# Cross-attention kernel, first layer: how the turned probabilities are copied out of PSUM, and the order of work at the layer's two ends

## What is computed

```python
q = hidden @ Wq + bq                    # 32 heads x 16
k, v = enc @ Wk + bk, enc @ Wv + bv     # 8 heads x 16
scores = einsum('bkgld,bksd->bkgls', q, k) * scale + mask
attn = softmax(scores, axis=-1)
out = einsum('bkgls,bksd->bkgld', attn, v)        # -> b, l, 512
x = out @ Wo + bo + hidden
x = (x - mean) * rsqrt(var + eps) * gamma + beta
...                                               # two cross-attentions, MLP
```

## Time and profile before

| | us |
|---|---|
| median of 3 runs | 2570.73 (2568.63 to 2571.31) |
| the profiled execution's own time | 2569.06 |
| its span | 2567.3 |
| PE busy | 2496.2 (97%) |
| DVE busy | 1699.2 (66%) |
| ACT busy | 1496.0 (58%) |
| first scores to last copy of the first layer, batch 0 | 31.75 to 261.47 |
| the same, batch 1 | 1307.63 to 1538.11 |

### The profile page before, as it was taken

The page is one execution under the profiler, slowest core; times in us unless marked ns, Lnnn a source line. Parts: engine busy times, 40 slices in busy tenths (PEclk is TensorE's granted clock), DMA queues, the critical chain, the costliest instruction groups (busy, mean ns, idle before and its releaser), DMA issues.

```text
span 2567.3 us, 53214 instructions
## 1 busy us (share of the span) xinstructions
PE 2496.2 (97%) x19500; PEld 2063.5 (80%) x19500; DVE 1699.2 (66%) x2568; ACT 1496.0 (58%) x2360; POOL 1324.9 (52%) x778
## 2 busy tenths in 40 slices
PE   8999999999999999999989989999999999999999
PEld 6666788888888888888866667888888888888877
DVE  7999675666566666665279996666666665666541
ACT  6999455554555555545469994555555455554543
POOL 1255356655644666555603543566566356655644
PEclk9999999999999999999999999999999999999999
DMA  6322034544514355352463210454454134544522
GB/s 205 83 85 70 34 101 112 130 118 109 126 42 101 101 128 131 100 127 68 148 155 91 64 67 33 103 130 128 100 129 112 36 101 120 130 110 118 128 66 66
DMA packets 87685, 263.62 MB, mean 103 GB/s; under 512 B 21312, under 2 KB 27088, under 8 KB 81888
## 3 DMA queue, kind: packets, MB, share of 16 engines
q1 hardware_dynamic: 86528, 260.80, 38.2%
q10 hardware_dynamic: 992, 0.52, 0.1%
HBM read 135.39 MB, written 8.40 MB: 56 GB/s over the span
## 4 chain that ended last, share of the span: by engine, by line
PE 81%; DVE 10%; issue 4%; ACT 2%; POOL 1%; DMA 1%; SPq 1%; DVEq 0%; POOLq 0%; ACTq 0%
PE ps_m L1109 22%; PE ps_t L1109 19%; PE ps_s L1109 17%; PE ps_m L1380 7%; PE ps_t L1380 6%; DVE sm L1720 6%; PE ps_s L1232 3%; DVE pt L1728 2%; PE ps_m L1313 1%; PE ps_m L1119 1%; POOL pT_lo L561 1%; PE ps_m L1271 1%; DVE nm L1720 1%; PE ps_t L1251 1%; ACT p L849 1%
## 5 line engine op out<-in xcount | busy, mean ns | idle before, releaser
L561 POOL TENSOR_TENSOR pT_lo<-pT_lo,pT_hi 128x1024 fp32r<-128x1024 f32 x220 | 529.5, 2407 | 498.1 <-ACT pT_hi L757 487.3
L757 ACT ACTIVATE pT_hi<-pT_lo 128x1024 fp32r<-128x1024 f32 x224 | 237.8, 1061 | 325.3 <-DMA pT_lo<-pb 325.3
L900 ACT ACTIVATE p<-ps_s,nm 128x1024 f32<-128x1024 f32 x256 | 284.9, 1113 | 207.1 <-DVE nm L1789 206.6
L1786 DVE TENSOR_REDUCE nmx<-ps_s 128x1 f32<-128x1024 f32 x256 | 309.7, 1210 | 122.1 <-PE ps_s L1109 122.1
L1109 PE MATMUL ps_s<-kT,qT 128*128 128x512 f32 x1536 | 383.7, 392 | 0.1
L1805 DVE STREAM_TRANSPOSE pb<-p 128x1024 f32<-128x1024 f32 x224 | 278.0, 1241 | 106.8 <-ACT p L900 102.7
L1109 PEld LDWEIGHTS ps_s<-kT,qT 128*128 128x128 f32 x1536 | 281.4, 188 | 55.7 <-ACT p L900 0.7
L1720 DVE CUSTOM_DVE_ANT_0 sm<-ps_s,mask 128x1024 f32<-128x1024 f32 x256 | 302.3, 1213 | 7.3 <-PE ps_s L1232 5.6
L849 ACT ACTIVATE p<-sm,nm 128x1024 f32<-128x1024 f32 x256 | 293.4, 1146 | 17.4 <-DVE nm L1720 13.5
L1109 PE MATMUL ps_t<-ctxT,wa 128*128 128x512 f32 x1080 | 256.0, 390 | 0.0
L1109 PE MATMUL ps_m<-hT,wa 128*128 128x512 f32 x1008 | 243.9, 393 | 0.9 <-ACT g L1071 0.7
(11 more groups left out here) (181 smaller groups left out, 4655.4 us busy)
## 6 DMA issues: line engine op xcount, KB each, us to landing
pT_lo<-pb SPq DMA_DIRECT2D x896, 128.0 KB, 2.3
stg_qk<-in_wqk SPq DMA_DIRECT2D x40, 1024.0 KB, 7.4
stg_vo<-in_wo SPq DMA_DIRECT2D x48, 512.0 KB, 3.6
wob<-in_wo SPq DMA_DIRECT2D x32, 512.0 KB, 3.6
stg_vo<-in_wv SPq DMA_DIRECT2D x32, 512.0 KB, 3.6
q_stack<-scr_q SPq DMA_DIRECT2D x36, 128.0 KB, 4.2
st_ctx<-in_ctxT SPq DMA_DIRECT2D x8, 512.0 KB, 6.3
mask<-in_mask SPq DMA_DIRECT2D x8, 512.0 KB, 6.4
```

What stands on the lines that cost most here:

```text
L561: return nc.gpsimd.tensor_tensor(out, x, f32(hi), ALU.subtract)
L757: return nc.scalar.activation(out, in_, ACT.Copy)
L900: nc.scalar.activation(p[t % 2][:], ps_s[t % 2][:], ACT.Exp, bias=nm[:, i:i + 1], scale=SCALE1, accum_out=sums[:, i:i + 1]).then_inc(exp_d ...
L1786: nc.vector.tensor_reduce(nmx[:, i:i + 1], ps_s[t % 2][:], AX.X, ALU.max, negate=True)\
```

## The change

It does five things, all in the first layer, and moves or merges work without changing what is computed.

1. **Paired copy.** The two `ps_t` banks become one PSUM tensor of 1024 columns (`ps_pair`), and the eight `pt0` buffers one SBUF tensor. `bank_of_half` becomes (2, 0, 2, 1): the upper half of an even step goes to bank 0, that of an odd step to bank 1, and the lower halves of all steps to bank 2. DVE's two copies of 512 columns become one of 1024 (`copied_pair`), issued when the odd step's upper half is there; it counts 2 on `t0_copied[1]`, at its end.
2. **Fourth Q tile.** `project_q0(3)` moves from before the first scores to behind them; ACT's `wide(b, 5)` moves behind the first two exponentials and DVE's `low_part(5)` behind the maxima of steps 2 and 3.
3. **First Q read.** The store of the first tile is split: the first 128 tokens have their own DMA and semaphore (`scr_q_first`). Of the six reads that the first scores need, SP issues three and ACT three.
4. **Output projection.** It goes into the four banks of `ps_s` (`out0_bank`), so no tile waits for DVE. Two of its sixteen matmuls are issued early: one in the last pair where the next pair's scores would stand, one behind the last transpositions.
5. `add_out` reads the new banks.

```diff
--- before
+++ after
@@ -141,7 +141,8 @@
         loop0 = at[0]
         sm = sb("sm", [P, S], F32, 2)
         p0 = sb("p0", [P, S], F32, 2)
-        pt0 = sb("pt0", [P, ST, P], F32, RING)
+        pt_ring = sb("pt0", [P, RING * ST, P], F32)
+        pt0 = [pt_ring[:, i * ST:(i + 1) * ST, :] for i in range(RING)]
         small_at = at[0]
         nm0 = sb("nm0", [P, 2], F32)
         z0 = sb("z0", [P, 2, UNIT], F32)
@@ -207,7 +208,8 @@
         assert max(ends) <= nc.sbuf_usable_end, (max(ends), nc.sbuf_usable_end)
         ps_s = [ctx.enter_context(nc.psum_tensor(f"ps_s{i}", [P, S], F32)) for i in range(2)]
-        ps_t = [ctx.enter_context(nc.psum_tensor(f"ps_t{i}", [P, 512], F32)) for i in range(2)]
+        ps_pair = ctx.enter_context(nc.psum_tensor("ps_t", [P, 2 * 512], F32))
+        ps_t = [ps_pair[:, i * 512:(i + 1) * 512] for i in range(2)]
         ps_m = [ctx.enter_context(nc.psum_tensor(f"ps_m{i}", [P, 512], F32)) for i in range(2)]
         ring1 = [*ps_t, *ps_m]
@@ -289,7 +292,7 @@
         bank0 = [ps_m[0][:], ps_m[1][:], ps_s[0][:, 0:512], ps_s[1][:, 0:512],
                  ps_m[1][:], ps_m[0][:]]
         turn_banks = [*ps_t, ps_m[1]]
-        bank_of_half = [(0, 1, 2, 0, 2, 1, 0, 2)[h % 8] for h in range(2 * STEPS0)]
+        bank_of_half = [(2, 0, 2, 1)[h % 4] for h in range(2 * STEPS0)]
         def half0(t, q):
@@ -311,6 +314,10 @@
         def unit_inverse0(u):
             return ps_m[0][:, u % 2 * 2 * P:u % 2 * 2 * P + 2 * P]
+
+        def out0_bank(lt):
+
+            return ps_s[lt // 2][:, lt % 2 * 512:(lt % 2 + 1) * 512]
         def turned_in(x, q, lt):
@@ -360,6 +367,11 @@
                 for e in range(2):
                     engine.dma_start(f32(k_stack[stack_rows(e, j), kps, i * 512:(i + 1) * 512]), src[e][:, kps, :])\
                         .then_inc(done, 16)
+
+        def first_q(engine, e):
+            for j in range(len(Q_ORDER)):
+                src = scr_q[0, :, Q_ORDER[j], 0:P].rearrange("(e g d) n -> e d g n", e=2, d=HD)
+                engine.dma_start(f32(q_stack[stack_rows(e, j), 0:GROUPS, 0:P]), src[e]).then_inc(stack_in, 16)
         @block.sync
         def _(sp):
@@ -428,15 +440,21 @@
                     if i >= 2:
                         after_group(i - 1)
                     sp.wait_ge(part_done, b * 6 + i + 3)
-                    sp.dma_start(scr_q[i, :, :, :], f32(parts[(i + 2) % 3][:])).then_inc(scr_q_out, 16)
+                    if i == 0:
+                        sp.dma_start(scr_q[0, :, :, 0:P], f32(parts[2][:, :, 0:P])).then_inc(scr_q_first, 16)
+                        sp.dma_start(scr_q[0, :, :, P:L], f32(parts[2][:, :, P:L])).then_inc(scr_q_out, 16)
+                    else:
+                        sp.dma_start(scr_q[i, :, :, :], f32(parts[(i + 2) % 3][:])).then_inc(scr_q_out, 16)
                     if i == 0:
                         sp.wait_ge(scr_k_out[1], 16 * (b + 1))
                         apart()
                         stack_k(sp, 1, slice(0, 1), stack_in)
+                        sp.wait_ge(scr_q_first, 16 * (b + 1))
+                        apart()
+                        first_q(sp, 0)
                     sp.wait_ge(scr_q_out, 16 * (b * 4 + i + 1))
                     apart()
                     if i == 0:
-                        stack_q(0, stack_in, slice(0, P))
                         stack_q(0, stack_next, slice(P, L))
                     else:
                         stack_q(i, stack_rest)
@@ -832,8 +850,11 @@
                                          bias=cols0[:, 5:6]).then_inc(v0_biased, 1)
                 act.wait_ge(scr_k_out[0], 16 * (b + 1))
                 stack_k(act, 0, slice(0, 1), stack_in)
-                for i in range(3, 6):
-                    wide(b, i)
+                wide(b, 3)
+                act.wait_ge(scr_q_first, 16 * (b + 1))
+                act.sem_inc(apart_act, 1)
+                first_q(act, 1)
+                wide(b, 4)
                 t0 = b * STEPS0
@@ -865,6 +886,7 @@
                 exp0(0)
                 exp0(1)
+                wide(b, 5)
                 for t in range(1, STEPS0, 2):
                     copied0(t - 1, 0)
                     if t + 2 < STEPS0:
@@ -1209,9 +1231,8 @@
                         st = 4 * i + s
                         mm = nc.tensor.transpose(ps_t[i][:, s * P:(s + 1) * P], vT0[:, st * P:(st + 1) * P], ident[:])
                     mm.then_inc(v0_turned, 1)
-                for i in range(2, 4):
-                    pe.wait_ge(w0q_lo, CT * b + i + 1)
-                    project_q0(i)
+                pe.wait_ge(w0q_lo, CT * b + 3)
+                project_q0(2)
                 pe.wait_ge(stack_in, 16 * 18 * (b + 1))
@@ -1278,7 +1299,13 @@
                         nc.tensor.transpose(inverse0(u), r0[u % 2][:].rearrange("p h d -> p (h d)"),
                                             ident[:]).then_inc(rb0_filled, 1)
+                def attended(lt, c):
+                    return nc.tensor.matmul(out0_bank(lt), aT0[:, c, lt * P:(lt + 1) * P], w0o[:, c, :],
+                                            start=c == 0, stop=c == KVP - 1)
+
                 scores0(0)
+                pe.wait_ge(w0q_lo, CT * (b + 1))
+                project_q0(3)
                 scores0(1)
                 turned0(0)
                 turned0(1)
@@ -1290,11 +1317,17 @@
                         pe.wait_ge(stack_rest, 16 * 54 * (b + 1))
                     if r + 1 < PAIRS0:
                         scores0(r + 1)
+                    else:
+                        pe.wait_ge(max0_done, t0 + STEPS0)
+                        pe.wait_ge(w0o_in, 16 * KVP * (b + 1))
+                        pe.wait_ge(a0_done, u0 + (KVP - 1) * LT + 1)
+                        attended(0, 0)
                     turned0(t - 1)
                     if t >= GROUPS:
                         for i in (t % GROUPS - 1, t % GROUPS):
                             values0(t // GROUPS * GROUPS - GROUPS, i)
                     turned0(t)
+                attended(0, 1)
                 for i in range(4):
                     values0(STEPS0 - GROUPS, i)
@@ -1304,14 +1337,11 @@
                         .then_inc(row1_filled, 1)
-                n0 = nb + U_PROJ0
-                pe.wait_ge(w0o_in, 16 * KVP * (b + 1))
                 for lt in range(LT):
-                    pe.wait_ge(a0_done, u0 + UNITS0 - 1 + (lt > 0))
-                    free(n0 + lt)
-                    for c in range(KVP):
-                        mm = nc.tensor.matmul(ps_m[(lt + 1) % 2][:], aT0[:, c, lt * P:(lt + 1) * P], w0o[:, c, :],
-                                              start=c == 0, stop=c == KVP - 1)
+                    if lt >= 1:
+                        pe.wait_ge(a0_done, u0 + (KVP - 1) * LT + lt + 1)
+                    for c in range(2 if lt == 0 else 0, KVP):
+                        mm = attended(lt, c)
                     mm.then_inc(bank_filled, 1)
@@ -1720,13 +1750,14 @@
                     nc.vector.tensor_tensor_reduce(sm[i][:], ps_s[i][:], mask[:, lt, :], -1.0, 3.0e38,
                                                    ALU.add, ALU.min, nm0[:, i:i + 1]).then_inc(max0_done, 1)
-                def copied0(t, q):
+                def copied_pair(t):
                     if t >= RING:
                         dve.wait_ge(pv0_done, b * (STEPS0 // GROUPS) + t // GROUPS - 1)
-                    dve.wait_ge(t0_filled[q], t0 + t + 1)
-                    nc.vector.tensor_copy(pt0[t % RING][:, :, TILE * q:TILE * q + TILE],
-                                          half0(t, q)[:].rearrange("p (s n) -> p s n", s=ST)).then_inc(t0_copied[q], 1)
+                    dve.wait_ge(t0_filled[1], t0 + t + 1)
+                    slot = (t - 1) % RING * ST
+                    nc.vector.tensor_copy(pt_ring[:, slot:slot + 2 * ST, TILE:2 * TILE],
+                                          ps_pair[:].rearrange("p (s n) -> p s n", n=TILE)).then_inc(t0_copied[1], 2)
                 def inverse(u):
                     dve.wait_ge(exp0_done, t0 + (u + 1) * UNIT)
@@ -1736,7 +1767,6 @@
                 for t in range(2):
                     maxima0(t)
-                low_part(5)
                 for t in range(1, STEPS0, 2):
                     if (t + 1) % UNIT == 0 and t < LT * UNIT - 1:
                         dve.wait_ge(mask_rest, 16 * (b * (LT - 1) + (t + 1) // UNIT))
@@ -1745,8 +1775,9 @@
                         maxima0(t + 1)
                     if t + 2 < STEPS0:
                         maxima0(t + 2)
-                    copied0(t - 1, 1)
-                    copied0(t, 1)
+                    if t == 1:
+                        low_part(5)
+                    copied_pair(t)
                     if t % UNIT == UNIT - 1:
                         inverse(t // UNIT)
@@ -1756,7 +1787,7 @@
                 def add_out(lt):
                     dve.wait_ge(bank_filled, n0 + lt + 1)
-                    nc.vector.tensor_tensor(x_res[:, lt, :], ps_m[(lt + 1) % 2][:], x_res[:, lt, :], ALU.add)\
```

(2 more changed lines are left out.)

## The result

The changed kernel takes 2648.57 us (median of 4 runs, 2642.3 to 2650.22) against 2569.73 for the kernel before in the same set of runs: ratio 1.03, interval 1.0287 to 1.0312. It is 79 us slower. The forecast had the sign and the mechanism, and 46 us; the measured time lies 14 us above its range.

A forecast was written before the change was run, and what follows sets the result against it. DVE was taken to bound the first-layer loop, PE a close second. Loop, start and end summed as 48.6 - 0.8 - 1.6 = +46.2 us, giving 2617 us, range 2598 to 2635.

The forecast's parts named there:

- the ring: First-layer loop: copy, even step's transpositions, values, odd step's transpositions, copy wait on each other without overlap; 3.88 us.
- I take 3.92 us a pair: First-layer loop: forecast time per pair with the paired copy, against 3.51 before, 0.41 more.
- 1.34 + 1.69 + 0.85: First-layer loop: 1.34 us from copy to waiting matmuls; the others span even-step transpositions through values and odd step, 2.54 together.
- rows 7: Earlier trace at the loop's end, without scores or maxima as cover; source of the 2.54 and 0.81 us.
- The unit's transposition: First-layer loop: turning the unit's sums, once in four pairs, adds 0.26 us there, or 0.06 a pair.
- Rival C: First-layer loop: the clock falls, a pair takes some 5.5 us, +250 us if it stayed, 2820; chance 0.04.
- The start: Before the first paired copy: scores at about 30.35 instead of 31.75, copy at 37.9 against 38.34; -0.4 us a batch.
- The end: Output projection: two early matmul calls give -1.72 us, the last pair's delays +0.96; -0.8 us a batch.
- Rivals A and B: First-layer loop: DVE stays the bound, 2559, chance 0.06; or half the loss, 3.65 us a pair, 2586, chance 0.05.
- the sum's own term on DVE: First-layer copies on DVE: a pair costs 1.135 us of issue instead of 1.20, saving 0.065.
- an upper ring of 4.00: First-layer loop: upper bound per pair, with a slower release and a unit transposition costing all of its 0.3 us.
- a cold start of +8: Loop start: upper bound of the start's share in the range, -4 and +8 us, for a clock falling later.

The follow-up runs named there:

- The two runs that part table, release and length: Changed kernel with two 512-column copies and the new table: 2569.93 us; the same with both banks released at the second copy's end: 2587.02 us.
- the first experiment: Changed kernel with the old bank table and two copies of 512 columns, both reordered ends kept: 2571.29 us, ratio 1.0004.

## Why the prediction was right or wrong

**That the ring closes, and the paired copy makes the loop slower: right.** DVE idles before each copy, PE before the even step's transpositions, the copy runs 1.225 us against the forecast's 1.22, and its issue takes 1.14 us. Taking the ring from the one place in the trace where no cover was left found the mechanism that DVE's full busy share hides. The two runs that part table, release and length confirm it piece by piece.

The pieces below are those of the profiled execution, which grew by 81.1 us where 46.2 were forecast. It is the slowest of the four; the median missed the forecast by 32 us.

**The size of the ring: too small by 0.155 us a pair, 17 of the 35 us missed.** The step that failed is "I take 3.92 us a pair"; measured are 4.08. One row of before is needed to lay its sum beside the result, the odd step's transpositions in the pair of the earlier trace rows:

```profile
259.93 0.14 PEld L1251 LDWEIGHTS ps_t<-ident,p 64*128 64x128 f32 x1 [0.21 <-issue]
```

Piece by piece, the forecast's 1.34 + 1.69 + 0.85 stand against 1.45 + 1.68 + 0.88. The first is the release: rows 7 gave the time from a copy to *values* (0.12 us behind its end), and the ring goes from the copy to *transpositions* (0.22). These stand behind a semaphore increment; a second one cost 0.15 us. The "very ring" was measured with another last link. The right link may have stood in the rows too: in the last pair of before, the first copy ended at 257.33 + 0.69 = 258.02 and the transpositions followed at 258.24, the same 0.22 later. PE waited there for an ACT copy as well, which ended at 258.10, so the rows don't decide it. On top I had shortened the sum by 0.02 because PE's phases in the hidden pair ran a little closer; they don't when each waits. The unit's transposition came out as said, 4.27 in every fourth pair.

**The first pairs and the clock: 12 us missed.** The forecast gave the first six pairs 3.95 us each; they took 4.4 in batch 0 and 4.7 in batch 1, 7 us more than forecast in all. The first pairs have no values, PE is busy for about half the time in them (1.94 of 4 us from 40 to 44), and the clock is 0.61 there and 0.50 from 44 to 48. I had argued that at the half clock PE would be nearly full. That holds with values (3.36 of 4 us from 44 to 48), and not in the pairs that have none. In batch 1 the slow place in mid-loop cost 4.5 us more (7.07 + 5.68 against 4.27 + 4.01), of which about 1 us is the pause. Rival C, the clock falling in the loop, had been priced at the whole loop or nothing; it came as a few short falls.

**The start: -0.8 forecast, +4.1 measured, 5 us missed.** The first scores came when forecast (30.56 for 30.35). What failed is "the fourth Q tile's 2.96 us now follow them": 2.96 is the time of that tile at the full clock behind other work. Behind 2.49 and 2.60 us of idling it took 4.13 and 4.57 in the two batches, and 4.99 behind 3.72 in the first experiment. Of the clock the prediction said that the moved tile fills a hole, and it didn't count the one that the move opens.

**The end: right.** -0.6 a batch for -0.8.

**Rivals A and B** fell: the two-bank copy runs at the pace of a one-bank copy, and the ring is 4.01 us and not under 3.44 or 3.65.

In the sum's own term on DVE, the copy's issue, the forecast was right: by the trace merging saves DVE 0.06 us of issue a pair, and none of it reaches the end. The Trainium skill's page Perfetto Trace Analysis (Optimizing Scalar/DVE Operations) gives about 125 ns of overhead for a DVE instruction on PSUM, twice that, and advises grouping where the engine is saturated. The same section of the Trainium skill speaks of breaking instructions up only where DVE is not saturated and causes bubbles on other engines. DVE was busy throughout before, so its advice pointed to grouping. Here keeping the two copies apart is worth 79 us, by the run with two copies and the new table.

**The range** failed because errors of one sign were added as if they could cancel: an upper ring of 4.00, a cold start of +8, "not all at once". They came all at once. The steady ring alone, 4.08 us at a clock of 1.00, lay above its bound. The first pairs and the start, which lost most by the lower clock, came on top; both stood behind idle stretches of PE that the change had opened.

## What to carry to other kernels

Before merging two instructions, ask what each released and when, and what each waited for: the merged one waits for the later producer and releases both at its end. If the two engines then alternate, and this ring is longer than either engine's own work, each added microsecond counts in full, however full the busy share of the merging engine looked before. When a wait becomes real, price its last link from a row with the same receiving instruction, its semaphore steps included. Where a move opens an idle stretch like the one here in front of matmuls, price them at both clock levels.

## What was not expected of the hardware

- A second semaphore increment in PE's queue between a wait and its matmul cost 0.15 us where the wait was real (release 0.37 us for 0.22), and nothing where PE was still working on earlier matmuls (1.69 us for 1.68 between the two steps' transpositions).
- From DVE's end of a copy to PE's transposition 0.22 us, to values, which have no increment, 0.12 us.
- Twelve matmuls of 512 columns took 4.13 us where PE had stood for 2.49 us shortly before, and 4.99 where it had stood for 3.72, instead of 2.96.
- At 0.72 busy (165.18 of 228.32 us) with gaps in every pair the clock stayed at 1.00 over all 56 pairs of one batch, and fell once in the other, for 10 us or so. PE had paused for 0.94 us in mid-transposition just before, with nothing that the profile shows to wait for; what caused the pause is open. In the run with the output projection and first read PE's weight loads paused for 1.90 us in mid-values before 1338.67, the pair took 4.92 us, and the clock stayed at 1.00.
